# Five-deep probability buffers and a separate instruction order for each engine in a macaron transformer layer

## The reference, cut to what matters

```python
x = x + 0.5 * ffn(layernorm(x))
x = x + attention(layernorm(x))
x = x + 0.5 * ffn(layernorm(x))

# ffn: one shared expert and 8 routed ones, hidden size 341, the best 4 of 8 by gate weigh in
gate = u @ Wg.T + routing_bias
weights = softmax over the 4 highest of gate, 0 elsewhere
out = swiglu(u, Ws1, Ws2, Ws3) + sum over e of weights[e] * swiglu(u, W1[e], W2[e], W3[e])
swiglu(u, w1, w2, w3) = (sigmoid(u w1.T) * (u w1.T) * (u w2.T)) w3.T

# attention: 16 heads of 64, causal, inner size 1024
q, k, v = split(u @ W_qkv); p = softmax(q k.T / 8, causal); out = (p v) @ W_out
```

## Time and profile before

| | us |
|---|---|
| median of 3 runs | 685.02 |
| lowest, highest | 684.95, 687.95 |
| span of the profiled execution | 683.0 |
| busy PE | 646.1 (95%) |
| busy DVE | 609.6 (89%) |
| busy ACT | 572.8 (84%) |
| busy POOL | 495.7 (73%) |

### The profile page before, as it was taken

The page is one execution under the profiler, slowest core; times in us unless marked ns, Lnnn a source line. Parts: engine busy times, 40 slices in busy tenths (PEclk is TensorE's granted clock), DMA queues, the critical chain, the costliest instruction groups (busy, mean ns, idle before and its releaser), DMA issues.

```text
span 683.0 us, 20985 instructions
## 1 busy us (share of the span) xinstructions
PE 646.1 (95%) x7846; PEld 414.1 (61%) x7846; DVE 609.6 (89%) x1701; ACT 572.8 (84%) x1110; POOL 495.7 (73%) x589
## 2 busy tenths in 40 slices
PE   5798989999999998999899999999999999999997
PEld 3465755465567565666566566665666567666665
DVE  4899799999998999899889999989999888789887
ACT  6789977898999888899978999997999997565654
POOL 3244775688899687788967889895789898566555
PEclk9999999999999999999999999999999999999999
DMA  7800000278799366588844788683678797100000
GB/s 205 258 1 1 1 2 1 54 111 148 120 129 154 57 104 120 100 140 123 145 75 79 114 140 141 125 137 56 102 125 134 144 144 110 33 1 18 17 2 16
DMA packets 226489, 62.97 MB, mean 92 GB/s; under 512 B 213202, under 2 KB 225620, under 8 KB 226388
## 3 DMA queue, kind: packets, MB, share of 16 engines
q1 hardware_dynamic: 226388, 61.64, 52.4%
HBM read 7.87 MB, written 1.05 MB: 13 GB/s over the span
## 4 chain that ended last, share of the span: by engine, by line
PE 45%; DVE 23%; ACT 16%; issue 9%; POOL 5%; DMA 1%; SPq 0%; ACTq 0%; DVEq 0%; POOLq 0%
PE bank L1068 13%; PE bank L1070 12%; PE bank L1069 12%; ACT probs L1424 6%; DVE probs L1710 4%; DVE glu L1619 3%; DVE xs L1649 3%; ACT glu L1386 3%; PE bank L1238 3%; DVE glu L1624 3%; POOL paired L1035 2%; ACT gluh L1407 2%; PE bank L1201 2%; POOL glul L1031 1%; ACT paired L1432 1%
## 5 line engine op out<-in xcount | busy, mean ns | idle before, releaser
L1031 POOL TENSOR_TENSOR glul<-glu,gluh 128x512 f16<-128x512 f32 x191 | 221.3, 1161 | 98.4 <-ACT gluh L1407 97.9
L1035 POOL TENSOR_TENSOR paired<-probs,paired 128x512 f16<-128x512 f32 x160 | 185.4, 1161 | 27.4 <-ACT paired L1432 24.5
L1386 ACT ACTIVATE glu<-bank,tanh_scale 128x512 f32<-128x512 f32 x167 | 113.3, 678 | 49.1 <-PE bank L1070 48.5
L1619 DVE SCALAR_TENSOR_TENSOR glu<-glu,bank 128x512 f32<-128x512 f32 x167 | 113.7, 681 | 24.8 <-ACT glu L1386 24.4
L1424 ACT ACTIVATE probs<-probs,exp_bias 128x128 f32<-128x128 f32 (+3 forms) x256 | 131.6, 551 | 3.6 <-POOL exp_bias L1043 3.5
L1710 DVE CUSTOM_DVE_ANT_0 probs<-bank,causal,score_scale 128x128 f32<-128x128 f32 (+3 forms) x256 | 128.0, 545 | 6.2 <-POOL paired L1035 5.0
L1068 PE MATMUL bank<-w3h,gluh 128*128 128x128 f16 x708 | 127.4, 220 | 5.9 <-POOL glul L1031 4.9
L1070 PE MATMUL bank<-w3h,glul 128*128 128x128 f16 x708 | 127.2, 220 | 0.0
L1069 PE MATMUL bank<-w3l,gluh 128*128 128x128 f16 x708 | 127.2, 220 | 0.0
L1407 ACT ACTIVATE gluh<-glu 128x512 f16<-128x512 f32 x191 | 118.5, 621 | 2.0 <-DVE glu L1624 2.0
L1624 DVE SCALAR_TENSOR_TENSOR glu<-glu,bank 128x512 f32<-128x512 f32 x167 | 114.7, 687 | 5.8
(11 more groups left out here) (236 smaller groups left out, 1619.8 us busy)
## 6 DMA issues: line engine op xcount, KB each, us to landing
pT<-paired SPq DMA_TRANSPOSE x160, 3.2
attention_raw<-in_L_attn_W_qkv SPq DMA_DIRECT2D x6, 256.0 KB, 5.3
xs<-in_L_attn_inputs SPq DMA_DIRECT2D x4, 256.0 KB, 4.7
vh<-in_L_ffn_W SPq DMA_DIRECT2D x6, 128.0 KB
pT<-in_L_ffn_W SPq DMA_DIRECT2D x6, 128.0 KB
out<-xs SPq DMA_DIRECT2D x3, 256.0 KB, 2.5
raw_more<-in_L_ffn_W SPq DMA_DIRECT2D x4, 128.0 KB
attention_raw<-in_L_attn_W_out SPq DMA_DIRECT2D x2, 256.0 KB, 6.4
```

Source lines behind the costliest of these rows:

```text
L1031: pool.tensor_tensor(glul[pair][:, :], g[:, :], gluh[pair][:, :], ALU.subtract).then_inc(glu_low)
L1035: pool.tensor_tensor(paired[n % PAIRED][:, 1, :], probs[n % PROBS][:, :], paired[n % PAIRED][:, 0, :], ALU.subtract).then_inc(probs_low)
L1386: act.activation(g[:, :], psum[b1.bank][:, :], ACT.Tanh, scale=tanh_scale[:, j:j + 1]).then_inc(tanh_made)
L1619: v.scalar_tensor_tensor(g[:, :], g[:, :], 1.0, psum[b1.bank][:, :], ALU.add, ALU.mult).then_inc(drained[b1.bank])
```

## The change

Three edits. First, PROBS, PAIRED and TURNED go from 4 to 5.

Second, four strings of letters, one letter for each step in which that engine's loop has a branch, give the order in which the engine takes its steps. A letter means "the next step of this kind, in the order of the list": steps of one kind never pass each other, steps of different kinds may. The list of steps itself, the banks and all semaphore counts stay as they are. SP keeps the list's order. For the first 69 steps of the list PE and POOL keep their order; ACT and DVE differ from it there in a few places, at measuring and weight-preparing steps above all.

Third, the norm's DVE part gets one more wait, `q.wait_ge(rstd_made, s["i"])`, for POOL's part of the norm before it.

```diff
-PROBS = 4
-PAIRED = 4
-TURNED = 4
+PROBS = 5
+PAIRED = 5
+TURNED = 5
...
+def in_turn(steps, engine):
+    waiting = {kind: deque(s for s in steps if s["kind"] == kind) for kind in KINDS.values()}
+    for letter in ORDER[engine]:
+        yield waiting[KINDS[letter]].popleft()
+    assert not any(waiting[KINDS[letter]] for letter in set(ORDER[engine]))
...
-            for s in steps:
+            for s in in_turn(steps, "gpsimd"):
...
-            for s in steps:
+            for s in in_turn(steps, "tensor"):
...
-            for s in steps:
+            for s in in_turn(steps, "scalar"):
...
-            for s in steps:
+            for s in in_turn(steps, "vector"):
...
                 elif kind == "norm_stats":
                     b = s["b"]
                     stream_ready(b, s["stream"])
+                    q.wait_ge(rstd_made, s["i"])
```

More of the change, by code:

```diff
@@ L671, in run @@
             pass
+KINDS = {
[9 rows of a table added]
+ORDER = {
+    "gpsimd": (
+        "LLLLLLnLLssfLsssssssssssnsssssWsWWsssWssWsssfnssWWsWssssssYbspbbppsbnppssbpbpyppbsspsbpubppssbpppbbp"
+        "usfppbsppbpbupssbpspbsupbppsbppsbpnppubssypbpsbpubsppppssnsussbsusybpssbppbppssbsbpppbppsupbbfppsbpp"
+        "spbupbpssbppspbsubppsbppbsuppbsssbppppbunbpspppbssypbupbssppnspssysssbuupbbspbppspsppbbspsbpspppubbf"
+        "sspbppubpbsppsbppspbbuppssbpppbsubpppbssppbunsbppspbspypubpsbpsnppssuyssssbsubbppspfpbpbsppbsspbpppu"
+        "bbssppsbpspbppbsuppbsspbppbupbsspnpbpsbuppsbppsbbuppsyspbpppbsbuspppsspsssfsussussssssssssnyssssssss"
+        "ssssssfsssssssssssssssssssH"
+    ),
+    "tensor": (
+        "BTTzTNgTGTNSTTGhhTSTTThdThhddhdGhTShTdddTThdThTdhddGhShTTTTdddhdRdhTdXhTzdhddTThhgddTdhhhhhddddhhdhd"
+        "ddhhdxhxdzhhdkhvhvvdddhvhqkhdqqvhdxqxkhdwqhdwqvwhdqwkhdwwdqhwqwvdhqkhwwdqxqwvwwhxgwwhqdkdhwddqqwwhqw"
+        "khdwwqhddqhwwwqkhxwxqhwqdwhwwoqhwdddqqwhhdwhwwwhdwhhwdxwkwvvwhvvxqdkdqhhvdddqqhkohqhwwqvhwdqkwwhdqxq"
+        "vghwwwqxddwwkhddwqhwvqhwdqkhwwwdqdwhqhwwxqkwhwxqdhqwwdhwwqkhdddwqqhowwqhwwddqwhqwhxwxwhwhhddhwkwwddv"
+        "hdwvvvhwddqkhqqvhxqkhogxqhdwwwqvhdddqkhwwdwqhqvhwwddqkwwhwqhxqvhwwxqwwkhddwqqhddwwqkwwhhdqqwhdwwqdkh"
+        "wwwqhwxqxhwwoqdwhqdwhdqwwhhddwwwhdhhwwdkvvhwwvvxqkgxqdhhddvqhddqkhoqhwqvdwhwqkhwwwdxqqxvhhwwdqkwwhdd"
+        "qqwvwhdwwqwkhqdhqhddwwwqkhxqwwwhxqwhwdqwkhwddwdqqhhwwowqwdhwddqqhhwhxwwwgxhhdwddhwwdhdwwhhdhdxhhxdhh"
+        "ddohhhddhddxhxhhhhdddhddddgxhhhhhxddhddhhhhhdhddxhxddddhhdhhddhhxhhxdddhhdhdhhddxHxddddd"
+    ),
+    "scalar": (
+        "BlCzNMMMNrPPPPMhsPhsPPhsPPPPshshMMhPshAhPPAMsshsPPshAPhsAAhAhPPPssAPAAhsslPPhhQsszshWsPPZhWsPhWPhhss"
+        "hsrWhhsWhsshWWshshhWslhszshhskhsvshvvhsvhsskheeppsvsheeppekheepphslpvyeheppkssheeppshsueevphpsepkehp"
+        "eepuvphseephrpepsskheesppusehpeepkhpepeshuepshpsepkehpeepuhpsesplyhessphepueepphephehspepshhsshksuvv"
+        "shuvvlykesehphseppsvheepksehpehssppveheppkehpuseepvsherppsepekshpepephuevphsepekphespeshusphepeepkph"
+        "sephuseephssepkhpeeppeshuspepeeppshlhyepesuhepphsshsephhueplkvhssysvvvhsuskheeppvheeppkheessrphesppv"
+        "heepesskphpeephpussvheeppekheppheupssvhepeepkhpssepehupeeppksehpheepsshuepspepkhepephuessheppeepsplh"
+        "eypheupsssephhepepshhushlykvvhsssvvkeuhshsrspvheeppkephsepehpepevsphepkheeepsppusvheehpsspkeheepppus"
+        "vsheeppskhepepheephpusepkhseepphsseupephlekphyepssuepehphepseeppheepushshepphepsssephhhrshsshuuhsssh"
+        "hsshhhshssshhsshsshhlyhhhssssshshhhrhssshhhhshssshhhsshsssshhhshhshsshsshhhhsshsshsssHMM"
+    ),
+    "vector": (
+        "nMMzgGrSUOOPPPPGhjPhSUPPhPPPMMMhPchhGPhSUPhPcMMMMhPhPPcGhhShUPPnPchRPXPhhchPzPhPcghQPPhhcrjhhhchhcnh"
+        "hhhczhhkhvchvvchvhmkhmmvnhmkchmhmvichmkhimchmvihmkihmmvihcgrjhmkihmmchimkhimchmihmkhimnhmichamihmmch"
+        "hicihhhnihkvvihvcmkmcvhhcmvhmkahmhmvihmkihmmvgrjichmkhimchmvhimkichmhmihmkihmchmihmkcihmnmhaimcihmnh"
+        "mhihcihhhcikvhcvvvihmkhmmvhmkhagrchmmvihcmjkihmhmvichmkhimhmvihcmkihmmhicmikhhmmchimkhimnhmihamcihmh"
+        "micnhhichhihkvvhivvmkcgmhhrjmvchmkhamchmvihmkihmmcvhihmkihcmmvhimikhmcmhhimkhnimhmichmkihmmchhaimcih"
+        "mmhhhiigchcrhijhichhhhhchchhahnhchhhchhhhchcghhhhchhhrhhccDDDDjhhhchhcchhhhhhhcchhchhhHccc"
+    ),
+}
```

## The result

The changed kernel takes 658.3 us (median of 4 runs, 658.05 to 660.57). The kernel before, beside it on the same chip, takes 686.4 us (4 runs, 684.95 to 687.95). The ratio is 0.9603 with a 95% interval of 0.9577 to 0.9628: 4.0% faster. The profiled execution's span went from 683.0 to 656.3 us, by 26.7 us. The prediction was a span of 669.5 (671.5 as a median) and a range of 660 to 686.

A forecast was written before the change was run, and what follows sets the result against it. PE was taken as the bound, with DVE close behind. Terms -5.7 (row mode), -11.2 (waits), -1.7 (clock) and +5.1 (new waits) gave -13.5 us: span 669.5, median 671.5, range 660 to 686.

The forecast's parts named there:

- Changes of row mode: On PE, 60 fewer switches between 128-row and 64-row matmuls at 0.095 us each: 5.7 us won.
- the bound of 0: Low bound of the row-mode gain on PE: nothing won if the freed time turns into waits.
- The clock: PE's granted clock dips after the wait near 272 us; a shorter wait there wins 1.7 us.
- The added wait and SP: DVE's extra wait for POOL's norm and SP keeping the list's order while POOL's changes: 0 us each.
- PE's waits: More PE work between producer and consumer shortens 14 of 22 PE gaps behind step 69: 11.2 us won.
- New waits on PE: Places on PE with closer bank reuse go from 16 to 35; 19 more at 0.27 us cost 5.1 us.
- Five buffers, "no gain of its own": DVE's 5.0 us of waits in front of probs may vanish, but DVE is not the bound: no separate gain.
- rival D: The buffers do nothing and the order acts alone; time as in the forecast, no separate chance given.
- C: Rival: nearly every PE wait goes, 28.1 us won, 656.9 us; chance 0.04.
- A: Rival: waits taken from one place reappear at the next full queue, 684.4 us, no change; chance 0.13.
- B: Rival: DVE's queue blocks at its head, making the kernel slower, 691.6 us; chance 0.17.
- the forecast's own signs: Profile after: PE idle near 11 us, busy about 5 us lower, POOL's route wait well under 14.8, more short glu waits.

The follow-up runs named there:

- one engine near the list: The change with ACT, POOL or DVE in turn put as near the list's order as the others allow: 708.7, 671.3 and 674.0 us.
- the one shared order: All four engines take one order, steps sorted by mean place in the four new orders, five buffers, against the kernel before: 680.3 us.
- the four-buffer orders: Against the kernel before: PE's new order, the other three as near theirs as four buffers allow; 684.0 us with four buffers, 664.9 with five.
- The first kernel in which POOL stands back: The change plus one wait: POOL holds one step before the router of pass 6 until DVE's subtraction is done; 656.0 us.
- the kernel with four stand-backs: The change plus POOL waits for DVE at four steps, before the router of pass 6 and at three norms; 654.3 us.

## Why the prediction was right and wrong

**Changes of row mode: right in size.** 60 fewer changes at 0.095 us were to give 5.7 us. The usual spacings fell by 6.6 us, and by 2.6 for 28 changes where nothing else was touched. In the change the freed time did not turn into waits. With 28 fewer changes in the list's order 1.9 of the 2.6 us did, and PE's new order alone has all 60 fewer and is slower. So the bound of 0 was a real danger, and the term came out because the waits went at the same time.

**The clock: right as far as seen.** The dip near 272 us is gone with the wait before it; what it was worth was not measured apart, and lies in the 18.0 us below.

**The added wait and SP: right**, to within 0.6 us: by distances between starts PE waits for the DMA of pT twice, 0.3 us each.

**PE's waits: this step failed.** It credited 14 of 22 places with 11.2 us, by how much PE work each string puts between the step that feeds a chain and the step that needs it. All 22 went (18.1 to 0.5 us), those credited with nothing too. The reasoning failed with the size: PE's new order alone has all that added work, and its waits rise to 37.0 us. How late a chain is depends also on where its pieces stand in the queues of POOL, ACT and DVE, and that I mostly took as given. With all four orders in place the chains come early, as the waits at route, expo, rstd and glu show; with the other three alone PE's waits are 65.8 us. The experiments with one engine near the list say that none of the four orders can be left out, and the one shared order kept the waits. Why these four fit each other, perhaps because an engine far behind PE is better off with another order than one close to it, was not tested.

**New waits on PE: this step failed.** It charged 19 more tight reuses of a bank at 0.27 us, 5.1 us in all. The 35 tight places cost 0.1 us together. The price came from 16 waits for DVE's glu in the trace of before, 4.3 us, and these were not the waits at the 16 tight places of then, which came to 2.7 us. At most of them DVE came to its glu straight from other work: the reader was late, whatever the distance. PE's new order alone has the same tight places as the change, and there they cost some 3 us by a like count. So a tight reuse costs where its reader is late, and with all four orders in place the readers were not. Waits, clock and new waits together were to give 7.8 us (11.2 + 1.7 - 5.1) and gave 18.0. These 10.2, the 0.9 by which the spacings gave more, and 2.1 of small excesses, start and end make up the 13.2 between the forecast span and the measured one.

**Five buffers, "no gain of its own": this step failed.** It held at the list's order (2.6 us) but not in the new ones, where the fifth buffer is worth 19.1 us. The chain of 7.2 us was weighed against 11.1 us of PE work between scores and weigh, which is not where the buffer binds: it binds on DVE and ACT, whose new orders run a unit further ahead and would stand at the head of their queues. That makes rival D wrong as well: these orders did not act alone. How much of the 28 us the exact orders would keep with four buffers can't be run.

**The rivals.** C came nearest in size, and the objection to it (DVE at 96%) was no objection: DVE ran at 95.7% and waited for little. A (waits come back) is close to how the shared order came out, and the slower side, B, is where the mixtures of old and new orders ended, 692.5 and 728.6 us; the change shows neither. Most of the forecast's own signs came, and larger than named: PE idle for 4.8 us where 11 was named, its busy time lower by 10.5 where 5 was, POOL at route 4.0 us. One did not: there were to be more short waits of PE for DVE's glu, and the row of PEld for it went from 16 waits to 5.

**What stays open**: which places within the orders matter. With five buffers, the 260 places by which the four-buffer orders differ from those of the change are worth 6.6 us (664.9 to 658.3); they were not taken apart.

## What to carry to other kernels

In a kernel like this, where four engines are 73 to 95% busy, try an order of its own for each engine, and change the orders together: here PE's alone, and the other three alone, were worse than none. Look for the buffer whose count the new orders run into: its price has to be read with those orders in place (19.1 us here), not with the old ones (2.6 us). Where one engine bounds the kernel, count its cheap hidden costs by distances between starts, since busy time hides them, look whether the freed time comes back as waits, and charge a tight buffer reuse only where its reader is late.

## What the runs showed of the hardware that was not expected

PE's longest wait after 50 us comes from one DVE instruction. The timeline of the changed kernel, DVE, POOL and PE from 540 to 548 us:

```profile
541.28 4.95 DVE L1645 TENSOR_TENSOR xn<-gate 128x256 f32<-128x256 f32 x1
546.15 0.18 DVE L1647 TENSOR_TENSOR shifted<-gate,top 128x32 f32<-128x32 f32 x1
546.26 1.11 DVE L1710 SCALAR_TENSOR_TENSOR xs<-bank,route,xs 128x128 f32<-128x128 f32 x4
547.29 0.67 DVE L1680 SCALAR_TENSOR_TENSOR glu<-glu,bank 128x512 f32<-128x512 f32 x1
...
540.30 1.19 POOL L1095 TENSOR_TENSOR paired<-probs,paired 128x512 f16<-128x512 f32 x1
541.42 2.30 POOL L1091 TENSOR_TENSOR glul<-glu,gluh 128x512 f16<-128x512 f32 x2
543.65 1.19 POOL L1095 TENSOR_TENSOR paired<-probs,paired 128x512 f16<-128x512 f32 x1
544.76 1.19 POOL L1091 TENSOR_TENSOR glul<-glu,gluh 128x512 f16<-128x512 f32 x1
...
548.02 0.39 PE L1128 MATMUL bank<-xnT,w1h 128*128 128x512 f16 x1 [2.38 <-DVE glu L1680]
```

The subtraction at L1645, whose inputs both lie in SBUF, takes 0.42 us as the median of its eight. Here it takes 4.95: it begins inside one of POOL's subtractions, and ends 0.3 us after the last of the four that POOL runs behind it without a pause. DVE did not get in between them. The collect and the glu behind it come late, and PE stands for 2.4 us. The Trainium skill, SBUF — State Buffer, Who interferes with whom, says that a VectorE instruction with two inputs in SBUF contends with a GpSimd instruction that reads SBUF, and that the order of issue decides which of the two blocks the other. The trace agrees: POOL was first, and DVE's 4.95 us end with POOL's run. With POOL near the list the same instruction took 5.02 us: it began at 551.88 us inside one of POOL's instructions and ended 0.3 us after the fourth behind that one.

The first kernel in which POOL stands back, DVE and POOL in the same stretch:

```profile
541.51 0.55 DVE L1647 TENSOR_TENSOR xn<-gate 128x256 f32<-128x256 f32 x1
541.98 0.18 DVE L1649 TENSOR_TENSOR shifted<-gate,top 128x32 f32<-128x32 f32 x1
...
542.24 2.28 POOL L1093 TENSOR_TENSOR glul<-glu,gluh 128x512 f16<-128x512 f32 x2 [0.46 <-DVE shifted L1649]
```

POOL gives 0.46 us and DVE gets 4.4 back; the median falls by 2.3 us. It does not always go so. In the kernel before, at 82.6 us, DVE's subtraction stands beside two of POOL's back to back, and ends a microsecond before they do, so there DVE got in between. DVE, then POOL:

```profile
82.59 1.03 DVE L1584 TENSOR_TENSOR xn<-gate 128x256 f32<-128x256 f32 x1
83.55 1.15 DVE L1586 TENSOR_TENSOR shifted<-gate,top 128x32 f32<-128x32 f32 x1
...
82.18 2.46 POOL L1031 TENSOR_TENSOR glul<-glu,gluh 128x512 f16<-128x512 f32 x2
```

What decides between the two cases stays open.

The same shows on small instructions with one input in SBUF. The changed kernel at 311 us, DVE and POOL:

```profile
310.87 1.20 DVE L1615 TENSOR_SCALAR var_eps<-moments 128x4 f32<-128x4 f32 x1
...
310.86 1.17 POOL L1055 TENSOR_TENSOR xn_pair<-xn,xn_pair 128x512 f16<-128x512 f32 x1
```

and the kernel with four stand-backs, where that instruction is done before POOL starts on the norm:

```profile
312.41 0.16 DVE L1619 TENSOR_SCALAR var_eps<-moments 128x4 f32<-128x4 f32 x1
...
312.65 1.16 POOL L1059 TENSOR_TENSOR xn_pair<-xn,xn_pair 128x512 f16<-128x512 f32 x1 [0.18 <-DVE var_eps L1619]
```

In the kernel before, the eight runs of the gate's subtraction took 1.27 us at most, and at that of pass 6 POOL stood idle in front of route. So an order that keeps POOL busy can take time from DVE at places that no semaphore shows. How often a fuller POOL does so was not tested: what DVE's instructions took over the shortest of their kind, counted from 0.3 us on, adds up to 5.7 us in the kernel before, 9.8 in the change (4.5 of it this one instruction) and 2.6 with four stand-backs.
